# A gated attention and expert layer: five terms of the head sum in one VectorE reduction, statistics of x on ScalarE

## The reference

```
x = x + tanh(g_xattn) * conv_mix(layernorm(x), k, bias, ctx, ctx)
x = x + tanh(g_ffn)   * experts(layernorm(x))

conv_mix(v, k, bias, x1, x2):            # 32 groups of 8 heads
    kv[i,j] = v[i] * x2[j]               # per batch, group, position
    y = causal_convolution(kv, k[group]) + bias * kv
    out[j] = sum over i of y[i,j] * x1[i]

experts(h): one of 8 experts per token, chosen by argmax of h @ router;
            (silu(h @ gate) * (h @ up)) @ down, with I = 1024
```

## Time and profile before

| | us |
|---|---|
| median of 3 runs | 676.66 |
| profiled execution | 673.78 |
| its span, first to last instruction | 672.1 |
| TensorE matmul busy | 641.4 (95%) |
| GpSimd busy | 554.7 (83%) |
| VectorE busy | 514.0 (76%) |
| ScalarE busy | 236.2 (35%) |

### The profile page before, as it was taken

The page is one execution under the profiler, slowest core; times in us unless marked ns, Lnnn a source line. Parts: engine busy times, 40 slices in busy tenths (PEclk is TensorE's granted clock), DMA queues, the critical chain, the costliest instruction groups (busy, mean ns, idle before and its releaser), DMA issues.

```text
span 672.1 us, 11021 instructions
## 1 busy us (share of the span) xinstructions
PE 641.4 (95%) x3203; PEld 532.9 (79%) x3204; DVE 514.0 (76%) x659; ACT 236.2 (35%) x346; POOL 554.7 (83%) x354
## 2 busy tenths in 40 slices
PE   7999999999999999989697999999999999999995
PEld 7787888888888887877586878888888888888874
DVE  6878888888888889778699959699999947550601
ACT  5444444333444443243131323333333332333321
POOL 2999999999999999848376878789889868786852
PEclk9999999999999999999798999999999999999998
DMA  7454555556565655457567646376666654451110
GB/s 219 126 192 153 181 187 179 189 189 189 189 189 189 189 173 158 173 207 265 176 217 255 217 148 227 117 232 217 218 216 207 232 165 156 157 157 46 46 50 18
DMA packets 51907, 117.77 MB, mean 175 GB/s; under 512 B 5901, under 2 KB 6093, under 8 KB 51889
## 3 DMA queue, kind: packets, MB, share of 16 engines
q1 hardware_dynamic: 43728, 99.68, 45.7%
q0 software_dynamic: 4320, 12.72, 5.3%
q10 hardware_dynamic: 3840, 5.15, 2.8%
HBM read 94.08 MB, written 25.02 MB: 177 GB/s over the span
## 4 chain that ended last, share of the span: by engine, by line
PE 68%; DVE 17%; POOL 6%; issue 5%; ACT 2%; DMA 1%; DVEq 0%; ACTq 0%; SPq 0%; POOLq 0%
PE pair L1467 25%; PE bank L1356 20%; PE bank L1483 13%; PE pair L1390 3%; DVE kv L1115 3%; DVE prod L1183 3%; PE pair L1326 2%; PE bank L1498 2%; POOL kv_lo L749 2%; DVE up L1270 2%; POOL sorted_x L497 2%; POOL prod L773 1%; DVE down_hi L1270 1%; PE bank L1440 1%; DVE prod L1151 1%
## 5 line engine op out<-in xcount | busy, mean ns | idle before, releaser
L1356 PE MATMUL bank<-kv_hi,strip 128*128 128x512 f32 x640 | 210.6, 398 | 0.1
L1356 PEld LDWEIGHTS bank<-kv_hi,strip 128*128 128x128 f32 x640 | 120.2, 188 | 25.2 <-issue 1.1
L749 POOL TENSOR_TENSOR kv_lo<-kv,kv_hi 128x2048 fp32r<-128x2048 f32 x30 | 138.4, 4612 | 2.2 <-issue 1.2
L1356 PE MATMUL bank<-kv_lo,strip 128*128 128x512 f32 x320 | 124.6, 389 | 0.0
L1151 DVE TENSOR_TENSOR prod<-bank,cT 128x512 f32<-128x512 f32 x128 | 84.9, 682 | 22.0 <-PE bank L1356 22.0
L926 ACT ACTIVATE kv_hi<-kv 128x2048 fp32r<-128x2048 f32 x30 | 57.6, 1920 | 111.1 <-DVE kv L1115 86.4
L1467 PE MATMUL pair<-up,xT_hi 128*128 (+1 forms) x288 | 90.0, 394 | 4.5 <-DVE up L1273 3.9
L1467 PE MATMUL pair<-gate,xT_hi 128*128 x288 | 91.5, 399 | 0.2
L1356 PEld LDWEIGHTS bank<-kv_lo,strip 128*128 128x128 f32 x320 | 60.3, 188 | 11.2
L1115 DVE TENSOR_TENSOR kv<-pair,cK 128x2048 f32<-128x2048 f32 x30 | 68.4, 2279 | 0.0
L1467 PEld LDWEIGHTS pair<-up,xT_hi 128*128 128x128 f32 x288 | 54.8, 191 | 16.7 <-issue 5.3
(11 more groups left out here) (193 smaller groups left out, 1159.1 us busy)
## 6 DMA issues: line engine op xcount, KB each, us to landing
raw<-gate_w SPq DMA_DIRECT2D x32, 512.0 KB
raw<-down_w SPq DMA_DIRECT2D x32, 512.0 KB
strip<-kparts SPq DMA_DIRECT2D x15, 1024.0 KB, 5.9
raw<-up_w SPq DMA_DIRECT2D x28, 512.0 KB
sorted_x<-fill SPq DMA_DIRECT2D x14, 792.0 KB, 4.6
xs<-sorted_x ACTq DMA_DIRECT2D x19, 256.5 KB
x_in<-x_back SPq DMA_DIRECT2D x16, 256.0 KB, 4.7
cK<-ctx_back SPq DMA_DIRECT2D x16, 256.0 KB, 4.8
```

Source lines behind the costliest of these rows:

```text
L749: nc.gpsimd.tensor_tensor(kv_lo[u][:, hh, :], kv[:, hh, :], kv_hi[u][:, hh, :].bitcast(f32), ALU.subtract).then_inc(s_klo, 1)
L1356: last = nc.tensor.matmul(y_bank[lb][:, :], strip[u][:, 2 * hh + t, d * P:(d + 1) * P], v[u][:, hh, mb * COL:(mb + 1) * COL], start=(mb == ...
```

## The change

The reduction of five blocks replaces the addition of two and three: VectorE sums blocks 0 to 4 in one `tensor_reduce` and writes block 7, and TensorE transposes block 7 alone. For that, `skip_last` writes block 4 (its values of `add_pairs` have been read by then, for which it waits) instead of 8. Groups 0 and 15 keep the old way. The sum and the sum of squares of x for groups 2 to 15 come from two ScalarE activations with accumulator output, and the root follows on the same engine; VectorE keeps the reciprocal and the bias.

```
 skip_last:
+                    slot = J if isinstance(g, int) and g in (0, G - 1) else J // 2
+                    if slot < J:
+                        eng.wait_ge(s_add, g + 2)
                     nc.gpsimd.tensor_tensor(
-                        prod[u][:, J, :].rearrange("p (a h j) -> p a h j", h=2, j=J),
+                        prod[u][:, slot, :].rearrange("p (a h j) -> p a h j", h=2, j=J),
 ScalarE:
+                def stats1(g, u, n):
+                    act.wait_ge(s_x[u], 16 * (n + 1))
+                    act.wait_ge(s_nb1, g)
+                    nc.scalar.activation(scrap[:, :], x_in[:, u, :], ACT.Identity, scale=-1.0 / L,
+                                         accum_out=nm1[:, 0:1]).then_inc(s_mean1, 1)
+                    act.wait_ge(s_mean1, g - 1)
+                    nc.scalar.activation(scrap[:, :], x_in[:, u, :], ACT.Square, bias=nm1[:, 0:1],
+                                         accum_out=sq1[:, 0:1]).then_inc(s_square1, 1)
+                    act.wait_ge(s_square1, g - 1)
+                    nc.scalar.activation(sd1[:, :], sq1[:, :], ACT.Sqrt, bias=eps_t[:, 0:1], scale=1.0 / L)\
+                        .then_inc(s_sd1, 1)
 stage of ScalarE, behind xn2T_out(g - 2) and ahead of kv_high(g + 1, 1 - u, 0):
+                    if known(g, lambda g: g < G - 2):
+                        stats1(g + 2, u, n + 1)
 ahead of norm1:
-                        root1(g + 2)
 ahead of the stages:
+                act.wait_ge(s_kout, 48)
+                act.wait_ge(s_const, 17)
 VectorE:
+                def ln1_last(g):
+                    dve.wait_ge(s_sd1, g + 1)
+                    wait(dve, s_xn, g)
+                    nc.vector.reciprocal(rs1[:, :], sd1[:, :]).then_inc(s_ln1, 1)
+                    dve.wait_ge(s_ln1, g + 5)
+                    nc.vector.tensor_scalar(nb1[:, :], nm1[:, 0:1], rs1[:, 0:1], 1.0, ALU.mult, ALU.mult)\
+                        .then_inc(s_nb1, 1)
 add_fours:
-                    nc.vector.tensor_tensor(prod[u][:, 0:2, :], prod[u][:, 0:2, :], prod[u][:, 2:4, :], ALU.add)\
-                        .then_inc(s_add2, 1)
+                    dve.wait_ge(s_skp, g + 1)
+                    nc.vector.tensor_reduce(prod[u][:, J - 1, :], prod[u][:, 0:J // 2 + 1, :].rearrange("p i t -> p t i"),
+                                            AX, ALU.add).then_inc(s_add2, 1)
 stage of VectorE:
-                        ln1(g + 2, u, n + 1)
+                        ln1_last(g + 2)
 sum_heads:
-                    terms = [0, 1, 2, 3, J] if five else [0, 1, J]
+                    terms = [0, 1, 2, 3, J] if five else [J - 1]
```

More of the change, by code:

```diff
@@ L233, in flamingo_layer_kernel @@
     hot = put("hot", [P, G + 1, E], bf16, att)
+    eps_t = put("eps_t", [P, 1], f32, att)
+    nm1 = put("nm1", [P, 1], f32, att)
+    sq1 = put("sq1", [P, 1], f32, att)
+    scrap = put("scrap", [P, L], f32, [down_at + slot + 4 * L])
     assert att[0] <= past_big
@@ L282, in flamingo_layer_kernel @@
         s_sd1 = sem("s_sd1")
+        s_mean1 = sem("s_mean1")
+        s_square1 = sem("s_square1")
         s_nb1 = sem("s_nb1")
@@ L726, in _ @@
                 nc.gpsimd.memset(xn_rows[:, G * (L + 1):], 0.0).then_inc(s_const, 1)
+                nc.gpsimd.memset(eps_t[:, :], EPS).then_inc(s_const, 1)
                 eng.wait_ge(s_kpart, 1)
@@ L1391, in sum_heads @@
                                                     prod[u][:, i, lb * P:(lb + 1) * P], ident[:, :],
-                                                    start=(i == 0), stop=(i == J), is_transpose=True)
+                                                    start=(i == terms[0]), stop=(i == terms[-1]), is_transpose=True)
                     last.then_inc(s_att, 1)
```

## The result

The changed kernel takes 726.21 us (median of 4 runs, 726.0 to 727.19) against 676.54 us for the kernel before on the same chip: 1.0733 of its time [1.0719, 1.0747]. The direction was forecast, the size was not: 681.9 us with a range up to 692. The profiled execution took 726.13 us, its span is 724.4. The two parts of the change, each made alone, account for it: the statistics on ScalarE alone take 1.0027 of the time before [1.0013, 1.0042], the reduction alone 1.0708 [1.069, 1.0727].

A forecast was written before the change was run, and what follows sets the result against it. GpSimd was taken to pace the kernel at 17.39 us a stage, with rings of waits giving 17.55 after. Start 2.2, stages 1.7 and end 1.3 add 5.2 to 676.7: 681.9 us, range 678.5 to 689, wider range 677.5 to 692.

The forecast's parts named there:

- The reduction, 2.81 us: VectorE's new sum of five blocks, 2560 elements: 2.81 us taken from contiguous VectorE rows, upper bound 6.6 from a GpSimd row.
- costly reads: Rival: jumping reads make the reduction 4.7 us, 19.4 us a stage, 707 us in all (705 by the page's rule); chance 0.13.
- The one-stage ring, 17.5 us: Waits from pair addition over skip product, reduction, second outer product, high part and low part to next pair addition: 17.5 us.
- the two-stage ring: Waits across two stages, over outer product, high part, GpSimd's low parts, reduction and TensorE: 35.1 us, 17.55 us a stage.
- GpSimd's idle time: In each stage, ahead of the first low part: GpSimd, with 16.6 us of its own, idles some 0.9 us.
- No turns taken: VectorE's reduction no longer alternates with GpSimd's skip product and the product behind it, freeing 0.93 us a stage on GpSimd.
- The wait of the skip product, 0.1: On GpSimd, the skip product waits for the pair addition: between nothing and 0.24 us, taken as 0.1.
- Statistics: Sums of x on ScalarE: about 2.3 us, hidden in the stages with 3 us to spare; start 2.2 us late.
- late high part: Rival: ScalarE's statistics need two table loads a stage or wait for x, delaying the high part; 688 us, chance 0.05.
- waits for x: Rival case on ScalarE: statistics wait for their input; with 2.6 added they take 4.9 us of 5.3 room; shared chance 0.05.
- The end, +1.3: Last stage, pair addition to expert choice: 1.9 us more for the longer chain, 0.6 less for a comparison, net 1.3.
- 1.7 us for the 13 stages: Thirteen convolution stages between first and last full pair additions, at 17.55 us each for 17.43: 1.7 us more.

## Why the prediction was right or wrong

**The reduction, 2.81 us: wrong.** This is the first step that failed. The prediction had bounds of 2.81 and 6.6 and took the lower "since it comes from the same engine". Its rows of VectorE were contiguous; the only row with a jump was GpSimd's, and it said that a jump costs. Measured 4.61, 1.75 ns an element against 1.04, near the half way point of 4.7 that stood in the rival. A rule of the Trainium skill had it (Vector Engine (DVE) Microarchitecture Reference, Measured stream behaviour on trn2): 1.73 ns a column for a source that hops every element. Its parenthesis, that a one-source operation alternating between two regions ran at full rate, does not carry over to this reduction. The 1.73 is from an operation of another kind with hops of 4 KiB; the 1.75 measured here, for a reduction of one source with hops of 2 KiB, agrees with it. By that rule the sum stood at 705; what is missing from 705 to 726 is the next step.

**The one-stage ring, 17.5 us: wrong, by a wait that was not read.** The prediction had the reduction reach GpSimd over the second outer product, the high part and the second low part. That is a wait with 2.28 + 1.92 us behind the reduction, and it was summed right. But `kv_low` (L743) waits for the sum directly, ahead of the first low part. In the kernel before that wait was over in time: GpSimd's low part at 125.67 came after the fours had ended at 124.99, and no idle time showed. The ring that it closes holds both low parts: from the earlier trace rows and the rows above, pairs 4.63, wait 0.07, skip product 1.08, 0.16 to the reduction, reduction D, 0.2 to GpSimd, low part, product, low part 9.94 to the next pair addition, so 16.1 + D. With 4.63 it is 20.7, as measured; with 2.82, 18.9, as in the experiment with contiguous reads. The rival "costly reads" had 19.4 and 707 us: the jump was priced, the ring was not. The kernel without the wait and with the clock kept is that rival, at 19.6 and 709.

**The two rings as summed, 17.5 and 17.55: right in size, the wrong one of the two taken as the pace.** With contiguous reads and no wait the stage is 17.66 and the time 7.4 us over its own before, where 5.2 was forecast. The forecast took the two-stage ring as the longer by 0.05. The trace has the one-stage ring, over the second outer product, as the tight one: GpSimd waits 0.41 us for the high part ahead of the second low part, and in that place the two-stage ring has 0.41 to spare. GpSimd's idle time was forecast at 0.9, all ahead of the first low part; it is 0.96, of which 0.55 stands there. That the pace came out right although the ring was the other one is luck of two sums that nearly agree. One small slip: 13 x (17.55 - 17.43) is 1.6, not 1.7.

**A third ring that was not formed.** It is the ring of VectorE and TensorE alone, by the rows above 4.00 from product 1 to the reduction, D, 0.05 and 0.43 for the head sums, 6.93, 0.78 and 2.34: 14.5 + D at full clock. At 2.82 that is 17.3, shorter than the others; at 4.63 it is 19.2, longer. Nor did it see that a pause of 2.8 us lowers the clock, which adds 1.6 us a stage to this ring (8.51 against 6.93); the run with spare transposes and without the wait shows that this lies on the path.

**No turns taken: right.** The product behind the skip product is at 0.96 instead of 1.86, with the reduction running beside it. The 0.93 us bought nothing, as forecast.

**The wait of the skip product, 0.1: right**, 0.07 in the stage shown and 0.17 in the first one.

**Statistics: right.** Two passes, two reads, a root: 1.9 us for 2.3, no table load in a stage, and 3.27 us of idle time left ahead of the high part. The start cost 1.6 for 2.2 (1.15 with the statistics alone), of which the table load is 1.28. Its rivals (late high part, waits for x) did not occur.

**The end, +1.3: too small.** It was 5.7. The first scatter starts 22.28 us behind the last full pair addition, where before it was 19.08 (294.36 - 275.28): 3.2, which is nearly the forecast 1.3 and the 1.8 by which the reduction is longer. Another 2.6 is the transfer of the last scatter on this chain, 5.44 us for 2.88. Why that transfer is longer stays open; no run isolated it.

**Shares.** The forecast had 1.7 us for the 13 stages and they cost 44.8, so the two failed steps are 43 us of the miss there. They can't be given separate shares: of the 49.7 us over its own before, contiguous reads alone give back 27.6, no wait alone 0.8, both together 42.2.

## What to carry to other kernels

Before an instruction grows, list every semaphore that it raises and every instruction that waits for it, also those waits that show no idle time in the profile: a wait that has always been over is invisible until the instruction is longer, and adding it to the ring is one sum. An operand with a jump is not priced by a contiguous row, not even of the same engine: here that row gave 2.81 us, another engine's row with a jump 6.6, and 4.61 was measured, so where the bounds lie that far apart, let the forecast and its range stand between them. When two rings are close, test the removal of both causes together; each alone shows next to nothing.

## What was not expected of the hardware

A VectorE reduction of 128x2560 with a jump of 2 KB at every element took 4.61 us, contiguous 2.82 us. A pause of 2.8 us in each stage left TensorE's granted clock at 0.50 for about two us behind it, and 30 matmuls took 8.51 us instead of 6.93; 22 useless transposes in the pause kept it at 1.00, and made the kernel without GpSimd's wait some 15 us faster. Each ScalarE activation with accumulator output was followed by an instruction that reads the accumulator, 0.18 to 0.19 us.
